# The last two items of an interleaved recurrent and expert kernel: an order of their own, and five passes on GpSimd

## The reference, cut to what matters

```python
def block(h, p):
    r = _retention(h, wk)                    # tril(q k^T) / row norm, divided by |row sum|, times v
    m = r @ w1 + b1
    a, gate = jnp.split(m, 2, axis=-1)
    m = a * jax.nn.silu(gate) @ w2 + b2
    m = _groupnorm1(m, gg, gb)               # one mean and variance over (tokens, features)
    y = m + h
    f = gelu(y @ wf1 + bf1_) @ wf2 + bf2_    # 128 -> 256 -> 128
    return (_layernorm(f + y, lg, lb), None)
...
s = _L0_attn_ref(xn, ...)                    # block, four layers
g = _silu(_L0_ffn_ref(xn, ...))              # per token one expert of 8: gelu(x @ w1[e] + b1[e]) @ w2[e] + b2[e]
x = x + s * g
```

## Time and profile before

| | |
|---|---|
| median of 3 runs | 503.05 us (502.96 to 504.04) |
| the profiled execution | 504.19 us, its span 502.1 us |
| mean granted clock of TensorE | 0.989 |
| TensorE, VectorE busy | 466.0 us (93%), 367.3 us (73%) |
| ScalarE, GpSimd busy | 262.2 us (52%), 262.0 us (52%) |
| moved by DMA | 37.15 MB |

### The profile page before, as it was taken

The page is one execution under the profiler, slowest core; times in us unless marked ns, Lnnn a source line. Parts: engine busy times, 40 slices in busy tenths (PEclk is TensorE's granted clock), DMA queues, the critical chain, the costliest instruction groups (busy, mean ns, idle before and its releaser), DMA issues.

```text
span 502.1 us, 9871 instructions
## 1 busy us (share of the span) xinstructions
PE 466.0 (93%) x3155; PEld 390.1 (78%) x3155; DVE 367.3 (73%) x1324; ACT 262.2 (52%) x548; POOL 262.0 (52%) x290
## 2 busy tenths in 40 slices
PE   6999889999999999999999999999999999988870
PEld 4887667666888889888988988988899888766540
DVE  4758878888768667777876777777677778766782
ACT  3823334445565545665554466654546655488530
POOL 4520188888444555454345555444555464445654
PEclk9999999999999999999999999999999999999995
DMA  9899811111511111111011111111111100231335
GB/s 262 239 130 215 333 38 32 39 38 57 112 66 54 42 60 64 59 58 38 33 63 41 66 58 59 44 37 53 40 63 59 39 7 10 86 95 22 43 42 63
DMA packets 47393, 37.15 MB, mean 74 GB/s; under 512 B 13336, under 2 KB 38752, under 8 KB 47312
## 3 DMA queue, kind: packets, MB, share of 16 engines
q1 hardware_dynamic: 40304, 28.93, 21.6%
q0 software_dynamic: 6512, 6.80, 6.7%
q10 hardware_dynamic: 528, 0.79, 0.5%
HBM read 16.79 MB, written 11.51 MB: 56 GB/s over the span
## 4 chain that ended last, share of the span: by engine, by line
PE 68%; POOL 13%; DVE 6%; issue 6%; DMA 2%; ACT 2%; POOLq 0%; SPq 0%; DVEq 0%
PE bank L1368 9%; PE bank L1290 7%; PE bank L1274 7%; POOL x_slots L480 6%; PE pair L1455 4%; PE pair L1426 4%; PE bank L1468 4%; PE bank L1301 4%; PE pair L1403 4%; PE bank L1302 4%; PE bank L1303 4%; PE pair L1457 3%; PE pair L1401 3%; PE bank L1366 2%; PE bank L1326 2%
## 5 line engine op out<-in xcount | busy, mean ns | idle before, releaser
L523 POOL TENSOR_TENSOR zhat<-zhat,all_lg 128x512 f32<-128x512 f32 x29 | 38.6, 1333 | 85.5 <-PE bank L1335 74.0
L1368 PE MATMUL bank<-all_f,G_sb 128*128 128x128 f32 x512 | 72.9, 275 | 0.0
L687 ACT ACTIVATE y_sb<-bank,gn_bi,gn_sc 128x512 f32<-128x512 f32 x32 | 24.9, 778 | 87.3 <-DVE gn_bi L1141 87.3
L1368 PEld LDWEIGHTS bank<-all_f,G_sb 128*128 128x128 f32 x512 | 67.3, 192 | 2.0 <-issue 2.0
L739 ACT ACTIVATE uT_h<-bank 128x512 fp32r<-128x512 f32 x32 | 19.1, 598 | 95.0 <-PE bank L1345 95.0
L1274 PEld LDWEIGHTS bank<-moe_w,h_T 128*128 128x128 f32 x312 | 39.5, 191 | 13.9 <-issue 13.9
L435 POOL TENSOR_TENSOR ln_rs<-ln_ve,half_neg 128x4 f32<-128x4 f32 x32 | 33.1, 1034 | 29.9 <-DVE ln_ve L775 29.6
L623 ACT ACTIVATE h_T<-bank,w_t 128x128 f32<-128x128 f32 x156 | 44.5, 372 | 5.1 <-PE bank L1290 5.1
L578 POOL DMA_INDIRECT y_rows<-yt,slot_info x39 | 41.0, 1050 | 11.1 <-POOL yt L575 11.1
L718 ACT ACTIVATE G_sb<-bank,all_par 128x512 f32<-128x512 f32 x64 | 42.8, 694 | 4.7 <-PE bank L1326 2.3
L545 POOL TENSOR_TENSOR gn_rs<-gn_ve,half_neg 128x1 f32<-128x1 f32 x32 | 18.9, 592 | 48.7 <-DVE gn_ve L989 48.6
(11 more groups left out here) (187 smaller groups left out, 1234.6 us busy)
## 6 DMA issues: line engine op xcount, KB each, us to landing
w_t<-moe_w SPq DMA_DIRECT2D x39, 258.0 KB
x_slots<-moe_w SPq DMA_DIRECT2D x1, 2515.5 KB, 20.6
xt<-x_slots SPq DMA_DIRECT2D x39, 64.0 KB, 1.8
x_sb<-in_L_attn_x SPq DMA_DIRECT2D x8, 256.0 KB, 5.8
moe_w<-in_L_ffn_w SPq DMA_DIRECT2D x1, 2048.0 KB, 19.0
moe_w<-y_rows SPq DMA_DIRECT2D x8, 256.0 KB, 5.1
out<-moe_w POOLq DMA_DIRECT2D x7, 256.0 KB, 4.6
all_f<-in_L_attn_Wf SPq DMA_DIRECT2D x2, 512.0 KB, 4.9
```

Source lines behind the costliest of these rows:

```text
L523: pool.tensor_tensor(zhat[:, b % 2, :, :], zhat[:, b % 2, :, :], all_lg[:, li, :].unsqueeze(1).broadcast_to([P, C, D]), ALU.mult)\
L1368: last = mm(dst[:, at_c], G_sb[:, k, at_c], all_f2[:, li, k, :], start=False, stop=k == 1)
```

## The change

Steps 0 to 29 stay as they are. Steps 30 and 31 and the three behind them are no longer made by `step` but by a list `ending()` on every engine. In it:

- the front of an item (query, scores, state sums, mask, outputs) stands in another place among the stages of the items before it, and `keep_warm` is gone;
- items 30 and 31 take value and gate as one plain float32 product each, from whole weights kept in `last_w` (`late_gate`, `late_value`), with no low part of u; their gate is ScalarE's Silu (`gate_silu`) in place of Tanh, Identity and the VectorE pass;
- the moments of items 29 to 31 come as three sums with the epsilon and the sign inside (`late_means`), so that VectorE takes two small steps and not three;
- `weigh` can be written by either engine. VectorE keeps "bias" of 5 and of 7 and "x" of 6; GpSimd takes "scale" of 7, 5 and 6, "bias" of 6 and "x" of 7. "x" adds x to the rows on the chip;
- items 6 and 7 are then stored by SyncE without adding, 7 in two halves; GpSimd stores 0 to 5 with adding, and the copy of x to `out` is only of these;
- item 31's second weight, residual, GELU, statistics and finish go in halves; its reciprocal deviation is ScalarE's Sqrt and VectorE's reciprocal, not GpSimd's power; its group sums are VectorE's;
- GpSimd fills three small constants at its start.

```diff
+        POOL_WEIGHED = (("scale", 7), ("scale", 5), ("scale", 6), ("bias", 6), ("x", 7))
...
+        def weigh(eng, done, what, b):
+
+            g = xn[:, b * C:(b + 1) * C, 0:D]
+            y = y_tok[:, b, :].rearrange("p (c d) -> p c d", c=C)
+            if what == "scale":
+                eng.wait_ge(scattered, 16 * NT)
+                eng.wait_ge(e_silu, SILU.index(b) + 1)
+                eng.tensor_tensor(g, y, all_lg[:, L - 1, :].unsqueeze(1).broadcast_to([P, C, D]), ALU.mult)\
+                    .then_inc(done, 1)
...
+            if what == "x":
+                weighed(eng, "bias", b)
+                eng.tensor_tensor(y, y, x_sb[:, b * C:(b + 1) * C, :], ALU.add).then_inc(done, 1)
...
-            sp.dma_start(out, x).then_inc(out_seeded, 16)
+            sp.dma_start(out[0:ENDING_B + 1], x[0:ENDING_B + 1]).then_inc(out_seeded, 16)
...
+                sp.wait_ge(dve_out, finished)
+                sp.dma_start(out[b, tokens].rearrange("(c p) d -> p c d", p=P),
+                             y_tok[:, b, tokens].rearrange("p (c d) -> p c d", d=D)).then_inc(out_stored, 16)
...
+            store(B - 2, slice(0, S), 2)
+            store(B - 1, slice(0, HALF), 3)
+            store(B - 1, slice(HALF, S), 4)
...
+                act.activation(th_sb[:, :], bank[3][:, :], ACT.Silu, bias=rowsT[:, column:column + 1]).then_inc(th_done, 1)
...
+                mm(bank[3][:, :], last_w[:, D:2 * D], uT_sb[:, :], start=True, stop=True).then_inc(pe_g, 1)
...
+                mm(bank[2][:, :], last_w[:, 0:D], uT_sb[:, :], start=True, stop=True).then_inc(pe_a, 1)
...
+                mm(pair[:, half, 0:HALF], all_w2[:, L - 1, :], gg_sb[:, half * HALF:(half + 1) * HALF],
+                   start=True, stop=True).then_inc(pe_w2, 1)
...
-            steps(pe, step, L, B, LAG)
...
+            steps(step, NO_TILES + 1)
+            ending()
```

More of the change, by code:

```diff
@@ L232, in need, with steps @@
                 eng.wait_ge(s, v)
[L234 to L240, removed]
+        def steps(step, count):
+            for s in range(count):
+                step(s // B, s % B)
         def at(l, t, late, width, count):
@@ new lines, in gelu, with last_gelu @@
+            def gelu(l, t):
+                if w := at(l, t, 2, B, LB):
+                    n, b, li = w
+                    if n == 0:
+                        act.wait_ge(fb_done, 1)
+                    for i, k in enumerate(halves(l, t)):
+                        act.wait_ge(pe_f1, n * 2 + i + 1)
+                        act.activation(G_sb[:, k, :], f1_bank(n, k)[:, :], ACT.Gelu,
+                                       bias=all_par[:, li, F_B + k:F_B + k + 1]).then_inc(G_done, 1)
+            def last_gelu(half):
+                part = slice(half * HALF, (half + 1) * HALF)
+                act.wait_ge(pe_f1, 2 * LAST + half + 1)
+                for k in range(2):
+                    done = act.activation(G_sb[:, k, part], bank[5 - half][:, k * HALF:(k + 1) * HALF], ACT.Gelu,
+                                          bias=all_par[:, L - 1, F_B + k:F_B + k + 1])
+                done.then_inc(G_done, 1)
@@ new lines, in last_residual, with last_deviation @@
+            def last_residual(half):
+                act.wait_ge(gn_affine, LAST + 1)
+                act.activation(y_sb[:, LAST % 2, half * HALF:(half + 1) * HALF], pair[:, half, 0:HALF], ACT.Identity,
+                               bias=gn_bi[:, :], scale=gn_sc[:, :]).then_inc(gn_done, 1)
+            def last_deviation(half):
+                chunks = slice(half * C // 2, (half + 1) * C // 2)
+                act.wait_ge(const_late, 3)
+                act.wait_ge(ln_var, LAST + half + 1)
+                act.activation(ln_sd[:, chunks], ln_mv[:, LAST % 2, chunks, 1], ACT.Sqrt, bias=eps_sb[:, :])\
+                    .then_inc(ln_dev, 1)
@@ L692, in step @@
                 s = l * B + t
-                if (not first or t < 2) and s != LB - 1:
+                if not first or t < 2:
                     queries(l, t)
@@ new lines, in scores, with outputs @@
+            def scores(n):
+                pe.wait_ge(q_done, n + 1)
+                for c in range(C):
+                    at_c = slice(c * P, (c + 1) * P)
+                    last = mm(pair[:, 0, at_c], hT[:, n % B, at_c], q_sb[:, at_c], start=True, stop=True)
+                last.then_inc(pe_A, 1)
+            def outputs(n):
+                pe.wait_ge(A_done, n + 1)
+                pe.wait_ge(S_done, n + 1)
+                for c in range(C):
+                    dst = pair[:, c // 2, (c % 2) * H1:(c % 2 + 1) * H1]
+                    last = mm(dst, A_sb[:, c, :], token_rows(n, c), start=True, stop=c == 0)
+                    if c:
+                        last = mm(dst, q_sb[:, c * P:(c + 1) * P], S_sb[:, c - 1, :], start=False, stop=True)
+                last.then_inc(pe_u, 1)
```

869 lines of the change are left out of this document (513 added, 356 removed).

## The result

The changed kernel takes 499.04 us (median of 7 runs, 497.53 to 501.38), the kernel before 503.78 us beside it (7 runs, 502.91 to 504.60); the ratio is 0.9916, 95% interval 0.9894 to 0.9937. I had forecast 495.8, with a range up to 499.0. The direction was right, and the time lies just outside the range.

What follows compares the result with a forecast made beforehand. Taken as bound: a chain of hand-overs between engines, then GpSimd's queue. VectorE's end at 488.7 + 0.1 + 2.4 landing + 3.6 wind-up gave span 494.8, 496.9 profiled, less 1.14 to the median: forecast 495.8 us, range 493.8 to 499.0.

Steps and rivals of the forecast that it cites:

- u(29) to u(30): Stretch between the transposes of u of items 29 and 30: 2.9 us saved by the new order, u(30) at 454.4.
- u(30) to u(31): Stretch between the transposes of u of items 30 and 31: 9.7 us of TensorE work, u(31) at 464.1, 4.3 earlier.
- GpSimd's queue: GpSimd's in-order list from 461.3: 17.5 us without a hole, gn_rs(31) at 477.7; of 4.3 us gained, 2.4 are left.
- The queue is the bound: Claim that GpSimd's list limits the ending by a little over 1 us, its power of item 30 coming after the variance.
- The last item: From the last y_sb to VectorE's end: 9.95 us in place of 11.0, from 478.8 to 488.7, 3.7 before 492.43.
- The rival that has the engines take turns: VectorE and GpSimd block each other from 457 to 478: 7.2 us lost, or 10.8 giving 506.6 us; chance 0.05.
- The counter that instructions reading PSUM are spared: Argument against that rival's price: half of VectorE's long instructions there read PSUM, which the lock leaves alone.
- The stores: After VectorE's end: a plain SyncE store of 128 KB landing in 2.4 us, then 3.6 of wind-up, ending at 494.8.
- wind-up: Time from SyncE's last landing to the span's end: 3.6 us (498.5 to 502.1), carried over unchanged.
- The table load for Sqrt: ScalarE's last table load, 1.28 us behind the last GELU, hidden ahead of the first half's variance; costed at nothing.

Runs made afterwards that it cites:

- e2: The changed kernel with all five passes that had moved to GpSimd put back on VectorE; median 497.32 us.
- e6: The gated kernel: e1 with GpSimd's list reordered and waits added, so no pass or store issue starts beside VectorE's chain from gn_rs to y_sb of item 30; 495.83 us.
- e1: The changed kernel with the pass "x" of item 7 moved from GpSimd to VectorE, behind the last y_sb; median 498.98 us.
- e5: The changed kernel with five filling products (keep_warm) put back into TensorE's waits behind 474 us; median 497.31 us.
- e9: The gated kernel (e6) with item 5 also stored plainly by SyncE and GpSimd's last store ahead of ln_rs(30); median 493.36 us.

## Why the prediction came out as it did

- **u(29) to u(30)**: right. u(30) started at 454.50 (forecast 454.4); mask first, and the 1.20 and 0.94 us of the earlier trace rows gone. Two small errors cancel in it: u(29) itself started at 444.17 in this execution, 0.35 late, and the step took 10.3 us where 10.6 were forecast (10.3 in e2 as well).
- **u(30) to u(31)**: right in mechanism. It was 465.37, not 464.1; ln_ve beside a row pass cost 1.0 on the way, and in e2, where that row pass ran earlier, it was 464.17.
- **GpSimd's queue, and the waits beside it**: this step failed. "The queue is the bound" rested on adding up its passes. But the last power there, gn_rs(31), waited 1.75 us for VectorE's gn_ve(31), and VectorE had been held up by GpSimd's passes, with 8.1 us of waits where 1.8 were charged. gn_rs(31) ended at 479.65, not 477.7, and a deliberate wait brought it to 476.6.
- **The last item**: 488.7 forecast, 493.2 measured. Charged to waits were 1.8 us, measured 8.1 by the rows above (0.9 of it, gn_bi of item 29, in slack). Of these 3.3 went by gating (e6), 2.3 by moving one pass (e1). The largest single one, "x" of 7 beside the finishing of item 30, I had costed as 0.69 us saved on VectorE and never placed in time. The rival that has the engines take turns named the mechanism and priced it at 7.2 us, the whole gain, and I gave it 0.05. The 7.2 came from nine passes at one price each, though; the 8.1 are seven meetings of 0.6 to 2.3 us, and 3.3 us of them, and ln_ve's 1.0, are with work that GpSimd had before. The counter that instructions reading PSUM are spared held (A_sb at 457.79 beside a "scale" pass, ln_st in e6; the A_sb of the earlier trace rows had only a store's issue beside it), but those on the chain between u and y are small and read SBUF. The rule of the Trainium skill that I cited there (SBUF — State Buffer, Who interferes with whom) is borne out: it covers gs and y_sb, which read two SBUF operands.
- **The stores**: the landing was 1.8, not 2.4 (1.8 to 3.0 over the runs). The 3.6 us of wind-up was mis-sized, since it was GpSimd's drain: 2.3 us in all behind VectorE, for 6.1. This error (3.8) hid most of the one above (4.5), so that the span, 495.5, came close to the forecast 494.8 for the wrong reasons.
- **The table load for Sqrt**: right. It took 1.28 us at 485.83, and the next activation started at 487.13, 0.02 us behind it, 3 us before the first variance. The further drain that the Trainium skill (ScalarE: Activation LUTs, What ACT_TABLE_LOAD costs) adds is not in the trace.
- **The clock**: not in the sum. keep_warm went with the change, and I did not price it. In e1 the clock stands at 0.50 for some 10 us of the ending; with the products (e5) the median is 1.7 us lower, by the ratios 3.1. I also subtracted 1.14 us, since the profiled execution of before was above its median; that of the change was 1.51 below. From the forecast 495.8 to 499.04 that is: 0.6 in the profiled execution (497.53 for 496.9), 1.1 and 1.5 in what stands between it and the median. So what carried the median out of the range is the spread of the executions, to which the sum gives nothing; the larger error, in the waits, was hidden by the one in the wind-up.

Open: whether a store's issue blocks VectorE. gn_bi beside one took 1.12 us at 472.41 and 0.22 without it (e6), but in the gated kernel the finishing of item 30 beside two of them took its 1.14. Nor is it known when the clock falls: executions of one kernel differ in it. And why the drain takes what it takes is not shown.

## What to carry to other kernels

A pass moved to an idle GpSimd is paid by whatever small SBUF instruction of VectorE starts beside it, so place it in time, against VectorE's chain, before counting what it saves; a deliberate wait on GpSimd can be worth more than the pass. Count GpSimd's end separately: in none of the 14 profiles did its drain end less than 5 us behind its last instruction, so where that sets the end, give the last stores, and the last power if it can be, to another engine. Where filling products are taken out, compare the spread of the runs and not one profile, and put them only into holes that are still there.

## What I had not expected of the hardware

- GpSimd's drain at the program's end: 5.1 to 7.7 us behind its last instruction, in 14 profiles; 6.3 behind a power of 128x4 in all three that ended with one.
- ln_ve, a TENSOR_SCALAR with one SBUF operand and a constant, 0.17 us alone, took 1.21 beside a row pass. Not only instructions with two SBUF operands wait.
- The executions of one kernel differ by up to 4 us (the change) or by 0.1 (e9): with the holes in TensorE's ending gone, the spread went too.
